# Decoder layer on one core: where the steady blocks wait for the stored keys, and where ScalarE fills the masked scores

## The reference, cut to what matters

```python
x = x + mamba(layernorm(x))                    # selective scan, 16 states, 1024 channels
x = x + attention(layernorm(x), ctx, pos, mask)  # 32 query heads, 8 key heads of 128
x = x + moe_lora(layernorm(x))                 # 64 experts of rank 8, top 16
# inside the first:
#   xc = silu(conv(x)); ssm = xc @ x_proj.T; dt, B, C = three rmsnorms of ssm
#   dt = softplus(dt @ dt_proj.T + bias); h = exp(dt*A)*h + dt*B*xc; y = h . C
# inside the second:
#   q, k turned by rotary tables; scores = where(mask == 0, -1e9, q.k / sqrt(128)); softmax; @ v
```

## Time and profile before

| what | value |
|---|---|
| runs of the kernel before | 2344.51, 2348.64 and 2348.67 us, median 2348.64 |
| the profiled execution: its own time | 2350.73 us |
| its span, first to last instruction | 2349.1 us |
| VectorE busy | 1762.5 us, 75% of the span |
| TensorE busy | 2086.0 us, 89% |
| ScalarE busy | 1003.9 us, 43% |
| GpSimd busy | 701.3 us, 30% |
| mean granted TensorE clock | 0.95 |

### The profile page before, as it was taken

How to read it: one execution, slowest core, us unless ns; L and a number is a source line. 1 busy time by engine, 2 the same in 40 slices (tenths; PEclk the granted TensorE clock), 3 DMA queues, 4 the chain that set the end, 5 groups by cost and what they waited for, 6 DMA issues and landing times.

```text
span 2349.1 us, 26708 instructions
## 1 busy us (share of the span) xinstructions
PE 2086.0 (89%) x8268; PEld 1192.0 (51%) x8272; DVE 1762.5 (75%) x1735; ACT 1003.9 (43%) x2549; POOL 701.3 (30%) x492
## 2 busy tenths in 40 slices
PE   6877887898999988998999989998999989799988
PEld 2333454345555543445556544345556544477774
DVE  4499994459999996259999996259999994456553
ACT  2544440265555532155545541255545540233331
POOL 0289992401111112401111111501111110456550
PEclk9788999889999999989999999989999999799999
DMA  2579895527888873435888874525887874332210
GB/s 63 165 178 230 210 215 169 146 95 175 176 182 196 184 180 101 154 117 135 186 190 179 186 166 119 186 91 136 190 190 181 188 166 117 103 99 90 86 59 18
DMA packets 117810, 352.12 MB, mean 150 GB/s; under 512 B 14016, under 2 KB 14144, under 8 KB 115296
## 3 DMA queue, kind: packets, MB, share of 16 engines
q0 software_dynamic: 40704, 146.82, 32.3%
q1 hardware_dynamic: 70112, 191.68, 26.6%
q10 hardware_dynamic: 6912, 12.59, 1.4%
HBM read 197.68 MB, written 23.33 MB: 94 GB/s over the span
## 4 chain that ended last, share of the span: by engine, by line
DVE 34%; PE 27%; DMA 17%; issue 14%; ACT 3%; POOL 2%; DVEq 1%; PEldq 1%; SPq 0%; POOLq 0%; PEld 0%; ACTq 0%
DMA xc<-hs 15%; DVE hs L1254 11%; DVE hs L1431 4%; PE acc L1753 4%; PE acc L1631 3%; DVE hs L1261 3%; DVE hs L1245 2%; PE pq L1684 2%; PE acc L1837 2%; PE pq L1714 2%; PE pq L1921 2%; PE pk L1921 2%; PE acc L1766 1%; DVE pzsc L1311 1%; DVE qr L1291 1%
## 5 line engine op out<-in xcount | busy, mean ns | idle before, releaser
L768 POOL DMA_DIRECT2D xc<-hs x192 | 164.1, 860 | 1116.3 <-DVE hs L1261 1095.9
L1254 DVE TENSOR_TENSOR_SCAN hs<-dA,hs 128x1024 f32<-128x1024 f32 x192 | 428.7, 2274 | 0.0
L988 ACT ACTIVATE dA<-dt,aneg 128x504 f32<-128x504 f32 x384 | 253.6, 707 | 320.0 <-DVE hs L1254 319.8
L1684 PE MATMUL pq<-qT,wa 128*128 128x512 f32 x768 | 354.1, 615 | 15.1 <-DVE pzsc L1311 14.9
L1766 PE MATMUL acc<-wb,oT 128*128 128x512 f32 x768 | 352.2, 603 | 3.6 <-ACT oT L976 3.6
L1261 DVE TENSOR_TENSOR hs<-hs,bc 128x1024 f32<-128x1024 f32 x256 | 307.6, 1203 | 2.2
L953 ACT ACTIVATE pr<-pzsc,mx 128x64 f32<-128x64 f32 x512 | 170.8, 335 | 245.1 <-DVE mx L1317 245.1
L1245 DVE TENSOR_TENSOR hs<-u,bc 128x1024 f32<-128x1024 f32 x192 | 227.5, 1217 | 26.6 <-DMA xc<-hs 21.0
L1631 PE MATMUL acc<-xnT,wa 128*128 128x512 f32 x512 | 234.4, 612 | 14.3 <-DMA wa<-in_wx 3.9
L1684 PEld LDWEIGHTS pq<-qT,wa 128*128 128x128 f32 x768 | 146.4, 196 | 189.3 <-issue 177.2
L1766 PEld LDWEIGHTS acc<-wb,oT 128*128 128x128 f32 x768 | 141.2, 193 | 148.0 <-issue 143.9
(11 more groups left out here) (255 smaller groups left out, 3379.2 us busy)
## 6 DMA issues: line engine op xcount, KB each, us to landing
xc<-hs POOLq DMA_DIRECT2D x240, 512.0 KB, 7.0
bc<-bc_rows SPq DMA_DIRECT2D x64, 512.0 KB, 7.5
wa<-in_wq SPq DMA_DIRECT2D x64, 512.0 KB, 10.2
wb<-in_wo SPq DMA_DIRECT2D x64, 512.0 KB, 7.0
wa<-in_wx SPq DMA_DIRECT2D x16, 512.0 KB, 7.0
wa<-in_wz SPq DMA_DIRECT2D x16, 512.0 KB, 3.8
wb<-in_ow SPq DMA_DIRECT2D x16, 512.0 KB, 6.3
wv<-in_wv SPq DMA_DIRECT2D x26, 256.0 KB, 13.1
```

Of the source, the lines that this page charges most:

```text
L768: G.dma_start(xc[:, 2 * c:2 * c + 2, :], hs[:, c, :].rearrange("p (d t) -> p d t", t=T), accum_op=ALU.add).then_inc(s_y[c], 16)
L988: ins = S.activation(to[:, :, 1:SEQ], dt[:, s, :].rearrange("p (b t) -> p b t", t=SEQ)[:, :, 1:SEQ], ACT.Exp, scale=aneg[:, s, bass.ds(jj ...
L1254: V.tensor_tensor_scan(out=hs[:, c, :], data0=dA[:, c % 2, :], data1=hs[:, c, :], initial=0.0, op0=ALU.mult, op1=ALU.add).then_inc(scd.sem, 1)
L1684: ins = M.matmul(pq[:, h, :], wa4(p)[:, k, h * P:(h + 1) * P], qT[:, k, :], start=(k == 0), stop=(k == KE - 1))
```

## The change

ScalarE's fill of `sc` moves in the steady passes from the head of the pass to just ahead of the first exponentials, behind the last Relu. VectorE, which before had no wait of its own for the stores, now waits for both `s_kst` semaphores behind `ssm_rows` and ahead of `rope_q(0, 0)`. Pass 4 (`not mamba`) is as before; no instruction's work changes.

```diff
@@ ScalarE, one() @@
-                if attn:
+                if attn and not mamba:
                     prefill()
                 if mamba:
                     eng.wait_ge(ssd.sem, ssd.upto(i, 0))
@@ ScalarE, behind the last Relu @@
                 if attn:
+                    if mamba:
+                        prefill()
                     exps(0, 0)
                     if not mamba:
                         swap_q(0, 1)
@@ VectorE, one() @@
                 if mamba:
                     ch = Chain(eng, ch_f, i)
                     ssm_rows(i)
+                if mamba and attn:
+                    for n in range(2):
+                        eng.wait_ge(s_kst[n], blk * 32 + 32)
                 if attn:
                     eng.wait_ge(s_mask, blk * 32 + 32)
                     eng.wait_ge(s_cs, blk * 32 + 32)
```

## The result

The changed kernel took 2333.95 us (median of 12 runs, 2325.71 to 2341.27); the kernel before, on the same chip, 2344.35 (median of 12, from 2339.09 up). One of those twelve took 8525.11 us and is left out of the ratio. The ratio is 0.9965, with a 95% interval of 0.9952 to 0.9977: faster by 0.35%, or 8.2 us, between 5.4 and 11.3. (The two medians lie 10.4 us apart; the ratio is the measure used here.) The forecast was 7.4 us of gain, but also 2341.2 us in a range of 2337.0 to 2347.5.

A forecast was written before the change was run, and what follows sets the result against it. Alternating stages were taken to set the end (VectorE 34%, TensorE 27%, transfers 17% of the last-ending chain). Pass 1 gains 4.71 + 2.71 = 7.42 us; 2350.73 less that is 2343.3, less 2.09 to the median 2341.2 us, range 2337.0 to 2347.5.

The forecast's parts named there:

- The sum of the gain: Pass 1, up to the first scan: 4.71 us of stall plus 2.71 us of TensorE speed, 7.42 us.
- carried through to the end undiminished: Behind pass 1's first scan: everything hangs on that scan, so the whole 7.42 us reaches the end.
- The stall: Pass 1, ScalarE: without the fill's wait the Square starts at 447.29 instead of 452.00, a gain of 4.71 us.
- What the idle gap does to TensorE: Pass 1, Square to first scan: without the gap TensorE's clock stays up, 76.33 becomes 73.62, gaining 2.71 us (0 to 3.79).
- VectorE's waits: Ahead of the first query product: stores land 8.4 us earlier in pass 1, so the new waits cost nothing.
- the fill's place: ScalarE, behind the last Relu: the 0.63 us fill costs nothing, since the scores release the mask later.
- the other queues: Pass 1: SyncE is free at 453.00, before its next transfer at 454.6; query weights and GpSimd's stores are unaffected.
- A: Pass 1 behind the Square: TensorE's clock stays low, 76.33 us again; gain 4.71, time 2343.9; chance 0.13.
- B: Pass 1's scan loop: falling into pass 2's pattern gives back 3.4 us; gain 4.0, time 2344.6; chance 0.17.
- C: Scan loops: VectorE's waits for state-adding transfers grow from 21.0 to 45.6 us; time 2365.8; chance 0.04.
- D: Pass 1: ScalarE is late for another reason, so the Square does not come forward; time 2348.6; chance 0.04.
- The rule of the Trainium skill: Square root's table load on ScalarE: about 1.38 us of drain would cut pass 1's gain by 0.7 us; left out.

The follow-up runs named there:

- experiments 1 to 4 and 6: In order: both kernels measured again unedited (1), VectorE's waits only (2), ScalarE's wait kept (3), other semaphore (4), VectorE's waits early (6).
- before, second: The kernel before, measured and traced again without any edit: 2344.71 us, ratio 0.9999.
- VectorE's waits only: The kernel before plus VectorE's two new waits, ScalarE's fill and wait staying at the head of the pass: 2340.99 us, ratio 0.9998.
- ScalarE's wait kept: The changed kernel with ScalarE's wait for the stores (s_kst[1]) put back at the head of the pass: 2339.36 us, ratio 0.9986.
- changed, second: The changed kernel, measured and traced again without any edit: 2338.23 us, ratio 0.9981.
- other semaphore: The changed kernel with ScalarE waiting at the head of the pass for s_kst[0], the earlier stores of pairs 0 and 2: 2337.11 us, ratio 0.9967.
- VectorE's waits early: The changed kernel with VectorE's two waits moved ahead of its rms rows: 2338.33 us, ratio 0.9978.
- experiment 5: Kernel before and changed kernel with passes 1 and 2 written out: 2331.69 and 2321.80 us; the former with five extra TensorE products in pass 1: 2328.11 us.

## Why the prediction was right or wrong

The table holds pass 1 of every looped trace in experiments 1 to 4 and 6, in us: the x_proj product's duration, from its end to the Square, from the Square to the first scan, from the product's start to the first scan, and from there to the end of the span.

| kernel | product | stall | Square to scan | product's start to scan | scan to end |
|---|---|---|---|---|---|
| before, first trace | 9.53 | 4.74 | 76.33 | 90.6 | 1820.8 |
| before, second | 7.08 | 6.64 | 75.16 | 88.9 | 1820.2 |
| VectorE's waits only | 7.08 | 7.31 | 74.59 | 89.0 | 1820.2 |
| ScalarE's wait kept | 7.08 | 6.61 | 74.92 | 88.6 | 1813.9 |
| changed, first trace | 7.08 | 0.03 | 74.32 | 81.4 | 1813.7 |
| changed, second | 7.08 | 0.04 | 74.32 | 81.4 | 1820.7 |
| other semaphore | 9.57 | 0.03 | 74.32 | 83.9 | 1821.4 |
| VectorE's waits early | 7.08 | 0.03 | 74.32 | 81.4 | 1824.2 |

**The sum of the gain: right.** With the product at full speed the way from its start to the first scan is 88.6 to 89.0 us with the wait and 81.4 without: 7.2 to 7.6 us, against 7.42 forecast. With the slow product it is 90.6 and 83.9, so 6.7. The first ratio's 5.4 to 11.3 us and the second's 0.7 to 8.2 hold that.

The table also takes apart the 18.2 us between the first two spans. At the first scan 11.1 us are there: 1.97 from an earlier start of the product, 2.45 from its speed, 4.71 from the stall and 2.01 from the Square to the scan. The other 7.1 arise behind the first scan, and are not the change's: the kernel with the wait kept is as quick there (1813.9), the second trace of the changed kernel as slow as the kernel before (1820.7). That the gain is carried through to the end undiminished is therefore not contradicted, but single traces, up to 10.5 us apart behind the scan, can't show it either; the ratios bear it out within their intervals.

**Its two terms: mis-sized, in opposite ways, and the sum right in part by luck.** The stall was put at 4.71 us and is 6.6 to 7.3 whenever the product isn't slow. What the idle gap does to TensorE was put at 2.71 us and comes to 0.3 to 0.8 at the first scan (74.59 to 75.16 against 74.32). The trace read beforehand had a slow product, which shortened the stall by some two microseconds, and the slowest start of all behind the Square (76.33). The 73.62 taken for the new pass 1, the middle of passes 2 and 3, was 0.7 us too low: pass 1 came out like pass 2, with the 28.4 us between the first two queries that experiment 5 shows, while pass 3 of the earlier trace rows has 72.54. Two errors of about two microseconds cancelled, which nothing in the prediction foresaw.

**VectorE's waits, the fill's place, the other queues: right.** Experiments 2 and 3 show it, and the rows above: 7.9 us to spare where 8.4 were forecast, a mask released by the scores, the same number of table loads. Passes 2 and 3 kept their distances, 74.32 and 72.51 us from Square to scan. The rms rows were ready at 450.2 and SyncE free at 449.0, closer than the 1.6 us forecast, but still in order.

**The step that failed** is the last of the sum: "It lies 2.09 above the median of the runs shown, 2348.64, so against that median I expect 2341.2". Three runs were taken for the kernel's level. Over 12 and 35 runs its median is 2344.35 and 2343.42, four to five below, and single runs lie 12 to 16 us apart in one set. Less 7.42 that gives 2336.9 or 2336.0, already at or below the range's lower end, 2337.0, to which only three microseconds had been granted for the spread of runs. The measured 2333.95 lies 3 us below 2336.9; the second measurement of the same kernel, 2338.23, lies 1.3 above it, inside the range. What sets these levels apart was not found.

**Rivals.** A, that TensorE stays cold: refuted by the 1.00 in the window behind the Square, and by experiment 5; in its price for the second term, nothing, it was still nearer to the 0.3 to 0.8 us than the 2.71 were. B, given back in the scan loop: it did not happen; the loops took 335.4, 337.0 and 334.5 us after, against 336.4, 339.8 and 335.4 in the earlier trace rows. C, slower by the adding transfers: VectorE's waits for them came to 5.2, 7.2 and 4.7 us, together 17.1 instead of 21.0, and the ratio refutes it as well. D, a Square late for another reason: refuted by its 0.03 us. The rule of the Trainium skill (ScalarE: Activation LUTs, What ACT_TABLE_LOAD costs) on the drain had been left out, rightly: in the changed kernel the root's table load starts at 443.48 and the root itself at 445.40, 0.64 us after the load's 1.28 us are over. Behind the load at 481.53 the first logarithm starts at 482.82, with 0.01 us between them.

**Left open.** Why unrolling gains its 10 us is not known. The traces place it: from the first scan of pass 1 to pass 2's x_proj product it takes 450.9 to 455.6 us in the eight looped traces and 446.7 and 447.8 in the two unrolled ones of experiment 5 without feeding, from there to pass 3's product 532.6 to 535.4 against 526.9 and 528.3. Right ahead of pass 2's product TensorE is idle for 2.3 to 4.1 us in the looped traces and for 0.84 in the unrolled ones, which is a part of it only. The moved fill without VectorE's waits was not tried, since then nothing orders VectorE's first query product behind the stores that read the same buffers.

## What to carry to other kernels

A wait belongs to the first instruction that needs what it protects; placed at the head of an in-order queue it holds up everything behind it, here a Square and with it a whole pass, while on VectorE it sat in idle time and was free. The cost of a wait for an outside event is the distance from the covering work's end to the event: if the covering work happened to be slow in the trace, the stall looks short, so read it against that work's usual duration. And a predicted level needs as many runs as a predicted difference: the difference here was right within 0.7 us in the traces, while the level was off by more than the range allowed.

## What the runs showed of the hardware

The same product of 16 matmuls took 7.08 us in six of these eight looped traces at pass 1 and 9.5 in two, with and without the change; in pass 2 of the same eight it ran 8.77 or 10.02 us in five. From the product's start to the Square the granted clock was 0.74 in the slow case of experiment 4 and 1.00 in the changed kernel. Which stretches run at the lower clock (1.2 GHz) thus differs from run to run of one kernel: the kernel before had a product of 9.53 us in pass 1 and 7.08 in pass 2 in one trace, 7.08 and 8.77 in the other. Single executions of one kernel lay 12 to 16 us apart in sets of 12 to 35.
